# Sums of squares of the attention's result, made by GpSimd in the FFN's steps

## The reference

```python
def _layernorm(x, axis=-1, eps=1e-05):
    m = jnp.mean(x, axis=axis, keepdims=True)
    v = jnp.var(x, axis=axis, keepdims=True)
    return (x - m) / jnp.sqrt(v + eps)

x = x + _L0_xattn_ref(_layernorm(x, axis=-1), ctx_4096, ctx_4096)
x = x + _L0_ffn_ref(_layernorm(x, axis=-1), L0_ffn_W, L0_ffn_b, L0_ffn_A, L0_ffn_B, L0_ffn_gate_w, L0_ffn_gate_b)
x = x + _L1_xattn_ref(_layernorm(x, axis=-1), ctx_4096, L1_xattn_conv_w, L1_xattn_bn_gamma, L1_xattn_bn_beta)
x = x + _L1_ffn_ref(_layernorm(x, axis=-1), L1_ffn_router_weight, L1_ffn_router_bias, L1_ffn_expert_bias)
```

## Time and profile before

| | |
|---|---|
| median of 3 runs | 3229.28 us (3222.10 to 3231.03) |
| the profiled execution | 3221.85 us, span in the trace 3220.1 us |
| mean granted clock of PE | 0.97 of full |
| busy share PE, DVE, ACT, POOL | 91%, 85%, 70%, 49% |
| attention, FFN, the rest | to 1278 us, to 2804 us, to 3220 us |

### The profile page before, as it was taken

One profiled execution on the slowest core, in us unless ns is written; L12 is line 12 of the kernel. 1 busy time (PEld: TensorE's weight loads), 2 busy tenths in 40 slices (PEclk: granted clock), 3 DMA queues, 4 the chain that ended last, 5 costly groups with the idle time before them and its releaser, 6 DMA issues. The chain is left out here.

```text
span 3220.1 us, 47965 instructions
## 1 busy us (share of the span) xinstructions
PE 2921.2 (91%) x13554; PEld 1595.2 (50%) x13554; DVE 2743.1 (85%) x7168; ACT 2258.1 (70%) x5947; POOL 1578.7 (49%) x1161
## 2 busy tenths in 40 slices
PE   5999999999999996899999999999999999838886
PEld 3666666666666664445444454444445444412332
DVE  4999999999999997676888979788897978778996
ACT  6878888888888763665675857667586766467773
POOL 5899989998999994001212112121211212015776
PEclk8999999999999998999999999999999999859997
DMA  5555555555555544354564737456473744453664
GB/s 196 173 178 159 162 176 171 159 165 175 169 159 167 176 125 149 104 148 140 154 195 131 211 112 205 151 155 186 134 216 107 205 151 129 111 198 146 246 250 165
DMA packets 272044, 532.26 MB, mean 165 GB/s; under 512 B 32664, under 2 KB 132760, under 8 KB 248992
## 3 DMA queue, kind: packets, MB, share of 16 engines
q1 hardware_dynamic: 245600, 422.17, 42.0%
q10 hardware_dynamic: 15168, 71.34, 7.8%
q0 software_dynamic: 11008, 35.66, 3.3%
HBM read 401.07 MB, written 128.02 MB: 164 GB/s over the span
## 5 line engine op out<-in xcount | busy, mean ns | idle before, releaser
L1057 PE MATMUL acc<-xh,wq 128*128 128x512 f16 x4096 | 1204.5, 381 | 45.7 <-DVE x_first L1714 16.4
L1057 PE MATMUL acc<-xl,wq 128*128 128x512 f16 x2048 | 758.1, 380 | 0.0
L1276 ACT ACTIVATE unused<-c_first,minus_guess 128x256 bf16<-128x256 f32 x1024 | 505.2, 494 | 266.5 <-DVE minus_guess L1588 224.1
L1057 PEld LDWEIGHTS acc<-xh,wq 128*128 128x128 f16 x4096 | 399.2, 98 | 530.6 <-DVE x_first L1714 22.0
L986 POOL DMA_DIRECT2D c_first<-ctx_pairs x120 | 66.4, 554 | 859.1 <-DVE mk L1639 848.7
L1057 PEld LDWEIGHTS acc<-xl,wq 128*128 128x128 f16 x2048 | 200.9, 98 | 243.1 <-issue 2.5
L439 PEld LDWEIGHTS bu<-m_iz,zf 128*128 128x128 f32 x2048 | 278.9, 191 | 49.9 <-issue 35.2
L439 PE MATMUL bu<-m_iz,zf 128*128 128x128 f32 (+2 forms) x2048 | 293.0, 301 | 4.7 <-DVE zf L640 4.7
L458 PE MATMUL bx<-m_ic,pf 128*128 128x256 f32 x1024 | 239.5, 387 | 35.2 <-POOL pf L343 35.2
L458 PEld LDWEIGHTS bx<-m_ic,pf 128*128 128x128 f32 x1024 | 191.7, 192 | 70.9 <-POOL pf L343 46.9
L1258 ACT ACTIVATE unread<-cf 128x256 bf16<-128x256 f32 x256 | 106.1, 415 | 129.1 <-DVE feat_pair L1687 92.7
(11 more groups left out here) (358 smaller groups left out, 7019.3 us busy)
## 6 DMA issues: line engine op xcount, KB each, us to landing
wq<-w_split SPq DMA_DIRECT2D x512, 256.0 KB, 3.2
c_first<-ctx SPq DMA_DIRECT2D x64, 512.0 KB, 6.8
xt<-xT SPq DMA_DIRECT2D x64, 512.0 KB, 6.4
x_pairs<-xo SPq DMA_DIRECT2D x64, 512.0 KB, 3.3
c_first<-ctx_pairs POOLq DMA_DIRECT2D x128, 256.0 KB, 4.7
x<-xn_pairs SPq DMA_DIRECT2D x32, 1024.0 KB, 5.6
out_pairs<-ost SPq DMA_DIRECT2D x32, 1024.0 KB, 5.0
x_first<-x SPq DMA_DIRECT2D x15, 2048.0 KB, 7.6
```

The costliest lines, as they stand in the source:

```text
L1057: return pe.matmul(acc[b][:], ws[(WQ * o + k // CK) % WR][:, k % CK, a, :], x[:, k, :], start=start, stop=False)
L1276: act.activation(signs[:, u // 2, t] if n == COUNTS - 1 else unused[u % 2][:], ct[k % CR][:, t], ACT.Sign, bias=guess[q % 2][:, u:u + 1], ...
```

## The change

The squares of the first pair (chunks 0 to 7, `SQUARED`) are made as before, in the attention. For all later chunks ACT's Square and POOL's `token_sums` are gone. `x1_squares` shrinks to one pair, `red2` is loaded once, and for pairs 1 to 7 POOL makes `red2` itself in the steps of the pair before, from the next pair's x in `xr`: `sums2`, chunk 0 at step 8, 1 at step 10, 2 at step 11 and 3 at step 13, one 128x512 multiply and 60 instructions of 128x256. The four matmuls on `red2` leave `gates` and become `tokens`, after tile 1 of the pair (for the first pair within tile 2), and write to `ps_b` in place of `ps_t`. Waits on `added_ok` and `sq1_ok` in the attention are capped at 8.

```diff
+    SQUARED = 2 * CH
...
                     if least(h, 2):
-                        sp.wait_ge(added_ok, h - 1)
+                        sp.wait_ge(x1_sum, CT * (h - 1))
+                        sp.wait_ge(added_ok, min(h - 1, SQUARED))
...
                 h = chunk(it, k, AFTER_I)
-                if h is None:
+                if h is None or h >= SQUARED:
                     return
...
-                if g is not None:
+                if g is not None and g < SQUARED:
                     s = (k - AFTER_I) % 2
                     act.wait_ge(x1_sum, CT * (g + 1))
                     act.activation(xt[s][:], xo[s][:], ACT.Square).then_inc(sq1_ok, 1)
...
+        SUMS2 = 1 + 4 * (KT - 1)
+        SUMS2_AT = {8: 0, 10: 1, 11: 2, 13: 3}
...
-                    if o == 8 and not is_last(i):
-                        sp.wait_ge(t_mm, i + 1)
-                        if isinstance(i, int) and i == NPAIR - 2:
-                            sp.wait_ge(sums_out[1], 16 * NPAIR)
-                        sp.dma_start(red2[:], x1_squares[bass.ds(i + 1, 1), :, :].rearrange("a p t -> p (a t)")).then_inc(r_in, 16)
...
+            def sums2(i, s, c):
+
+                at = SUMS2 * (i - 1)
+                pool.wait_ge(x_in[s][c], 16 * (i // 2 + 1))
+                for k in range(c * CK, (c + 1) * CK):
+                    if k == 0:
+                        pool.wait_ge(t_mm, i)
+                        pool.wait_ge(r_in, 16)
+                        pool.tensor_tensor(red2[:], xr[s][:, 0, :], xr[s][:, 0, :], ALU.mult).then_inc(sum2_ok, 1)
+                        continue
+                    for h in range(2):
+                        n, v, total = at + 1 + 4 * (k - 1) + 2 * h, xr[s][:, k, h * L:(h + 1) * L], red2[:, h * L:(h + 1) * L]
+                        pool.wait_ge(sum2_ok, n)
+                        pool.tensor_tensor(square[:], v, v, ALU.mult).then_inc(sum2_ok, 1)
+                        pool.wait_ge(sum2_ok, n + 1)
+                        pool.tensor_tensor(total, total, square[:], ALU.add).then_inc(sum2_ok, 1)
...
                     norm3(i, 1 - s, o)
+                    if o in SUMS2_AT and not is_last(i):
+                        sums2(i + 1, 1 - s, SUMS2_AT[o])
                     for im, _, _, om in mask_steps(i, s, u, o):
                         if (om >= GT or not first(im)) and om % GT >= 2:
                             load_next(im, om)
...
-                    pe.wait_ge(ready_ok, i)
-                pe.wait_ge(r_in, 16 * (i + 1))
-                pe.wait_ge(k_set, N_SET)
-                for q in range(QT):
-                    mm = pe.matmul(sq2[:, q:q + 1], red2[:, q * P:(q + 1) * P], ones[:, 0:1], start=True, stop=True)
-                mm.then_inc(t_mm, 1)
...
+            def tokens(i):
+
+                pe.wait_ge(r_in, 16)
+                pe.wait_ge(k_set, N_SET)
+                if not first(i):
+                    pe.wait_ge(sum2_ok, SUMS2 * i)
+                for q in range(QT):
+                    mm = pe.matmul(sq2[:, q:q + 1], red2[:, q * P:(q + 1) * P], ones[:, 0:1], start=True, stop=True)
+                mm.then_inc(t_mm, 1)
...
+                    elif o == LAG and first(i):
+                        main(i, o, {8: lambda: tokens(i)})
...
+                    if o == 1 and not first(i):
+                        tokens(i)
```

More of the change, by code:

```diff
@@ L357, in token_sums @@
                 if c == 0:
-                    if least(b, 2):
-                        pool.wait_ge(sums_out[bb % 2], 16 * (it + bb // 2))
                     pool.tensor_tensor(total[:], xt[s][:, 0, :], xt[s][:, 1, :], ALU.add).then_inc(added_ok, 1)
@@ L369, in token_sums @@
                     pool.wait_ge(added_ok, n_ready)
-                    pool.dma_start(x1_squares[bass.ds(it + bb // 2, 1), :, bb % 2 * L:(bb % 2 + 1) * L].rearrange("a p t -> p (a t)"), total[:]).then_inc(sums_out[bb % 2], 16)
+                    pool.dma_start(x1_squares[:, bb % 2 * L:(bb % 2 + 1) * L], total[:]).then_inc(sums_out[bb % 2], 16)
             def step(it, k):
@@ L390, in _ @@
             for s in range(2):
-                pool.wait_ge(sums_out[s], 16 * (NB // 2 - s))
+                pool.wait_ge(sums_out[s], 16)
         @block.tensor
@@ L598, in step @@
                         act.wait_ge(x1_out[s], 16 * (4 * it + kk // 2))
-                        act.wait_ge(sq1_ok, g - 1)
+                        act.wait_ge(sq1_ok, min(g - 1, SQUARED))
                     act.activation(xo[s][:, :, 0:P - 1], bu[:].rearrange("p b (h t) -> p (b h) t", h=2)[:, :, 0:P - 1], ACT.Copy).then_inc(odd_sb, 1)
@@ L731, in step @@
                         dve.wait_ge(x1_out[s], 16 * (4 * it + kk // 2))
-                        dve.wait_ge(added_ok, g - 1)
+                        dve.wait_ge(added_ok, min(g - 1, SQUARED))
                     dve.wait_ge(w_rec, g + 1)
@@ L853, in ffn_phase @@
         eps = sb("eps2", [P, 1])
+        square = sb("square", [P, L])
         red2, red3 = sb("red2", [P, T]), sb("red3", [P, T])
@@ L874, in ffn_phase @@
         w_rows = [ps_g, acc[2], acc[3], ps_b]
-        sq2 = ps_t[:, 2 * GC:2 * GC + QT]
+        sq2 = ps_b[:, 0:QT]
         x_in = [x_in_first, [sem(f"x1_in1_{c}") for c in range(NCH)]]
@@ L883, in ffn_phase @@
          st3_mm, std3, r3t_ok, rb3_mm, r3_ok, xn3_ok, cmax_ok, smax_ok, csum_ok, xsum_ok,
-         feat_ok, row_out, flag_mm, flag_ok, bn_ok, std_ok, guess_ok, off_ok, sign_ok, fin_ok, cut_ok, top_ok, kth_ok, mask_ok, bad_ok) = map(sem, (
+         feat_ok, row_out, flag_mm, flag_ok, bn_ok, std_ok, guess_ok, off_ok, sign_ok, sum2_ok, fin_ok, cut_ok, top_ok, kth_ok, mask_ok, bad_ok) = map(sem, (
              "k2_in", "w_sums_spread", "w_sums_ok", "w_sums_mm", "w_cols_ok", "gsum_mm", "gmean_ok", "g_centred", "g_hi", "g_lo", "lora_sum_ok", "lora_sum_mm", "lora_sums_ok", "aug_hi", "s_hi", "aug_ok", "ident16_ok", "red2_in", "k2_set", "x_hi", "x_lo", "x_lo2", "sq_ok", "part_ok", "sqsum_ok", "sq_fold",
@@ L887, in ffn_phase @@
              "st3_mm", "std3", "rstd3_ok", "r3_mm", "r3_ok", "xn3_ok", "cmax_ok", "smax_ok", "csum_ok", "xsum_ok",
-             "feat_ok", "row_out", "flag_mm", "flag_ok", "bn_ok", "std_ok", "guess_ok", "off_ok", "sign_ok", "fin_ok", "cut_ok", "top_ok", "kth_ok", "mask_ok", "bad_ok"))
+             "feat_ok", "row_out", "flag_mm", "flag_ok", "bn_ok", "std_ok", "guess_ok", "off_ok", "sign_ok", "sum2_ok", "fin_ok", "cut_ok", "top_ok", "kth_ok", "mask_ok", "bad_ok"))
         again = []
@@ L946, in _ @@
                 load_w(1, c)
-            sp.dma_start(red2[:], x1_squares[0, :, :]).then_inc(r_in, 16)
+            sp.dma_start(red2[:], x1_squares).then_inc(r_in, 16)
             def pair(i, s, u):
                 for o in range(OT):
-                    if o == 8 and not is_last(i):
-                        sp.wait_ge(t_mm, i + 1)
-                        if isinstance(i, int) and i == NPAIR - 2:
-                            sp.wait_ge(sums_out[1], 16 * NPAIR)
-                        sp.dma_start(red2[:], x1_squares[bass.ds(i + 1, 1), :, :].rearrange("a p t -> p (a t)")).then_inc(r_in, 16)
                     for c in range(WQ):
@@ L2517, in autocorrelation_lora_ffn_channel_attention_experts @@
     x1, xn3 = scratch("x1_pairs", pairs_shape), scratch("xn3_pairs", pairs_shape)
-    x1_squares = scratch("x1_squares", (NB // 2, P, 2 * L))
+    x1_squares = scratch("x1_squares", (P, 2 * L))
     masks = scratch("mask_pairs", pairs_shape, UINT8)
```

## The result

| | before | after |
|---|---|---|
| median | 3225.74 us (3222.10 to 3231.03, 4 runs) | 3352.12 us (3350.18 to 3353.70, 4 runs) |
| span of the profiled execution | 3220.1 us | 3351.7 us |
| FFN begins on POOL | 1278.04 | 1274.39 |
| first corrections of pair 2, of pair 8 | 1530.6, 2650.2 | 1535.7, 2781.0 |

The ratio is 1.039, 95% interval 1.037 to 1.041: 126 us slower. The forecast was 3355. The executions that the traces show lie 131.6 us apart (spans of 3220.1 and 3351.7 us).

What follows compares the result with a forecast made beforehand. DVE was taken to bound the attention and PE, delayed by DVE, the FFN. 6 x 19.3 + 12 - 2 = +126 us takes the profiled 3221.9 to 3348, plus 7 to the runs' median: 3355 us, range 3255 to 3400.

Steps and rivals of the forecast that it cites:

- Attention: End of the attention: without POOL's last store the barrier hangs on SP's last landing, some 2 us sooner; lighter POOL, ACT nothing.
- Length of POOL's blocks: FFN sums on POOL: chunk 0 takes 11 us, each other chunk 13 us, 50 us a pair.
- Locks: Chunks 0 and 1: DVE's two-tile instructions wait for POOL's, making the take of tile 10 8.0 us late; bounds 3 and 14.
- Late loads: Chunk 2 delays the second half of the context loads by 13 us, 12.2 eaten by slack: +1.1 us a pair.
- low_parts: DVE's two L1488 meet POOL's two L1007, both reading two SBUF tiles: +4.2 us a pair, bounds 0 and 8.
- Corrections: From take 13 to `low_rest`, DVE comes later than PE at the corrections: +6 us a pair, bounds 0 and 10.
- tokens: Waits for all 61 sums, which end about 2083, before PE is through tile 1: costs nothing, cover 6 us.
- First pair: First FFN pair, no features running: its late loads (13 us), low_parts and corrections put at 12 us.
- The sum of 19.3 us: Each of six FFN pairs: 8.0 for locks, 1.1 late loads, 4.2 low_parts and 6.0 corrections.
- dearer: Rival: PE's clock falls to 0.50 after waits, adding 5 to 7 us a pair: 3400 us; chance 0.12.
- the attention gives: Rival: POOL or ACT paces the attention after all, so its DVE idle time goes: 3182 to 3229, say 3195 us; chance 0.10.
- Only the loads count: Rival: locks cost little; late loads and 4 to 6 us at corrections remain, 7 x 7 = 49: 3276 us; chance 0.19.

Runs made afterwards that it cites:

- the kernel without sums: The change with the `sums2` calls and the wait of `tokens` for them taken out: 3223.73 us, ratio 0.9998 to the kernel before.
- chunks 0 and 1 alone: The change with only chunks 0 and 1 of the FFN sums made, at their places in the change: 3276.02 us, ratio 1.0165 to before.
- chunk 2 alone: The change with only chunk 2 of the FFN sums made, between the two halves of step 11's loads: 3278.75 us, ratio 1.0173 to before.
- no reads: The change with POOL writing constants for about the same time in place of the sums, reading no SBUF: 3292.85 us, ratio 1.0211 to before.
- Other places: The change with chunk 1 at step 12 ahead of POOL's low parts, chunks 2 and 3 at step 13 behind them: 3330.82 us, ratio 1.033 to before.
- the loads first: The change with the third chunk of sums moved behind both halves of step 11's context loads: 3283.33 us, ratio 1.018 to before.
- the first four runs: Variants of the change: sums removed, 3223.73 us; third chunk behind step 11's loads, 3283.33; constants written instead of sums, 3292.85; the last two edits together, 3225.84.

## Why the prediction was right

The time was right, 3355 against 3352, and so was the mechanism: sums beside features and ahead of loads make DVE late, and PE with it. That the two numbers lie so close is in part luck, twice over. PE's waits were put too high by about what the clock, which the sum left out, cost (below). And 7 us of the 3355 were the distance from the profiled execution of before to the median of its three runs; a fourth run made that distance 4 us, while the traces lie 131.6 us apart where the sum had 126.

- **Attention, -2 us.** -3.65 us at the start of the FFN. DVE paces it, as read from the earlier trace rows; the kernel without sums shows nothing more in it. ACT's Square stood, in effect, ahead of `co`, not `kf`; this changed nothing.
- **Length of POOL's blocks, 11 and 13 us.** 12.1 us for chunk 0 (2038.36 to 2050.48), 12.4 for chunk 2. The multiply, for which I took the add's 0.73, takes 0.61 when it reads one tile twice; the locks put back the difference.
- **Locks, 8.0 us late at the take of tile 10.** 9.4 with chunks 0 and 1 alone. The pitch of 0.81 is as worked out; 19 features met the blocks where I counted 11, and what I added for other instructions made up for that.
- **Late loads, +1.1 us.** On DVE the working was right: it put take 12 at 2058.4 in place of 2036.3, 22.1 us late, and it is 22.6 late in the table. That slack in front of PE eats most of chunk 2's part was right too: with chunk 2 alone take 12 is 10.8 us later than take 10, but PE's waits for takes come to 32.8 us in all, before 29.6. What that lateness does further on are the next two terms. The loads' effect as a whole I had at 1.1 + 4.2 + 6.0 = 11.3 us a pair; alone they cost 9.4 (chunk 2 only) to 11.6 (no reads).
- **low_parts, +4.2.** The collision is there in full (POOL's two 11.70 us in place of 8.11), but PE waits only 6.6 + 3.1 = 9.7 us for `xl` in the six pairs, 1.6 each.
- **Corrections, +6.** 16.5 + 16.0 us for `low_rest` and `rstd` in the six pairs, before 0.8 for `low_rest`: 5.3 a pair.
- **tokens, 0.** Right in the change. "Other places" shows the other side, where the cover of 6 us is gone: there PE itself is held, as the prediction said it would be.
- **First pair, 12.** 8.5.

Of the signs named beforehand, the pair of 205 to 210 us came (207.6 on average), and so did POOL's wait of 4 us before `zf`, features above 700 ns and L1488's instructions (now L1513) of over 4 us. PE waits for takes 10 us a pair, not 8; for `low_rest` 3, not 6, and for `rstd` another 3.

The sum of 19.3 us was for each of six pairs, and all of it waits of PE. These six pairs of the traces:

```profile
1530.64:2650.20 1119.56, 1099.85 (x5809) 529.45 (x5809) 937.12 (x2971) 772.55 (x2839) 214.79 (x156) 1.00 0.57 165
```

```profile
1535.66:2780.99 1245.33, 1142.32 (x5808) 540.30 (x5808) 1053.27 (x2971) 772.70 (x2838) 510.22 (x522) 0.96 0.50 147
```

Idle time grew by 13.9 us a pair: takes 7.0 (31.1 + 29.6 us, before 9.4 + 9.3) where I had 9.1, `xl` 1.6 where I had 4.2, corrections 5.3 where I had 6.0. **The missing part is busy time at the lower clock**, which the sum left out: PE is busy 42.5 us more for the same matmuls, 7.1 a pair. 13.9 + 7.1 = 21.0. I had this mechanism, but only in the rival "dearer", as 5 to 7 us on top of the forecast, with a chance of 0.12. Its size was right. It should have been a term, and the idle terms smaller.

PE at the lower level, two stretches between two corrections after (the third column from the right is the granted clock):

```profile
2276.94:2280.35 3.41, 3.06 (x8) 1.14 (x9) 3.07 (x10) 2.84 (x13) 1.90 (x3) 0.50 0.01 2
...
2362.27:2372.51 10.24, 7.52 (x27) 4.29 (x28) 8.45 (x37) 4.54 (x15) 1.02 (x2) 0.50 0.29 96
```

and PE in order of time at the first and the second of them:

```profile
2277.29 1.04 PE L1074 MATMUL acc<-xh,wq 128*128 128x512 f16 x2 [4.12 <-DVE x_first L1739]
```

```profile
2362.59 2.08 PE L1146 MATMUL ps_r<-ident,rstd 128*128 128x128 f32 x8 [3.75 <-DVE rstd L1549]
...
2367.07 0.61 PE L1161 MATMUL ps_g<-ident,low_hi 128*128 128x128 f16 x4 [2.40 <-DVE low_rest L1589]
```

0.50 is the 1.2 GHz level; it stands right at the end of waits of 4.12 us for a take and of 3.75 and 2.40 us at the corrections. Over the seven pairs the trace records this level for 108 us after and for 13 before, and PE is busy in 87 and 11 us of it. Matmuls take twice as long there: two of 128x512 last 1.04 us at 2277.29 above, as long as four do at the full level:

```profile
2119.13 1.04 PE L1074 MATMUL acc<-xl,wq 128*128 128x512 f16 x4 [1.34 <-POOL xl L1005]
```

So half of the busy time at this level is the clock's, and by this estimate (87 - 11) / 2 = 38 of the 42.5 us. That the clock fell because of the waits is argued from their place in time and from its going along with them: the mean is 0.99 with 27 us of idle time in seven pairs (before, 1309.74 less 1282.96), 0.96 with 119 (after, 1444.05 less 1325.41), and between them, with the loads first, 0.98 with 73:

```profile
1336.60:2715.80 1379.20, 1306.45 (x6752) 620.22 (x6752) 1149.27 (x3396) 889.50 (x3245) 552.84 (x605) 0.98 0.51 152
```

No run changed the clock alone.

The rivals: "the attention gives" fell by the kernel without sums. "Only the loads count" was half of the truth, and so were the locks; the additive result of the first four runs shows that neither would have done. The rule of the Trainium skill that the prediction cites (SBUF — State Buffer, "SBUF: two separate sides"), that the other engine fully blocks, against my reading that POOL keeps its pitch: both are seen. On pieces of 0.6 us POOL loses only 0.06 us each, on the `xl` pair, 4.07 us against 2.29, POOL's instruction takes 5.9, some 1.8 more, which is nearly all of DVE's. There the rule, not my reading of the earlier trace rows, is what the trace shows.

## What to carry to other kernels

Work that is moved to an engine because it is idle pays in two other places: what stands behind it in the same list, loads above all, and what another engine reads beside it. Price both by position: here a chunk of 11 to 13 us cost nothing, 5 or 9 us a pair, depending on where it stood. And when a sum gives waits of PE of some microseconds each, add a term for the clock behind them; here PE's longer busy time was a third of the loss.

## What the runs showed of the hardware

- A POOL instruction that only writes SBUF leaves DVE's feature instructions at their own pace (627 ns mean against 763 with reads, 645 before).
- POOL's multiply of a tile by itself is cheaper than an add of two tiles: 0.61 against 0.72 us for 128x256, 0.40 against 0.46 for 128x128, 1.04 for 128x512. From the three multiplies, about 0.21 us for each 128 columns and 0.19 fixed (an estimate). A multiply of two different tiles is not cheaper: 2.35 us for 128x1024, where the adds' 0.46 and 0.72 lead on to 2.3.
- The lock does not scale with the piece: delays at the same take of 4.8, 9.0 and 10.3 us for pieces of 0.40 to 0.46, 0.61 to 0.72 and 1.04 us, the last with a fifth less POOL time in all (35 us a pair in place of 45).
- A small instruction of DVE can be held as long as a large one: L1605 over 128x8, 0.17 us at the median, took 4.03 us and ended with POOL's second `xl`.
